# Value projection of two heads at once by halves, and the output's drain moved to ScalarE a turn later, in a two-layer transformer kernel

## The reference

```
q = x @ (wq_codes * scales) + bq;  k, v likewise          # 256 -> 16 x 128
scores = einsum("bqhd,bkhd->bhqk", q, k) / sqrt(128)
attn   = softmax(scores);  out = einsum("bhqk,bkhd->bqhd", attn, v)
return (out @ (wo_codes * wo_scales)) + bo
```

## Time and profile before

| | |
|---|---|
| time, median of 3 runs | 1179.99 us (1179.53 to 1180.14) |
| profiled execution, its own time | 1189.32 us |
| its span | 1187.5 us |
| PE, DVE, ACT, POOL busy | 88%, 63%, 47%, 24% of the span |
| chain that ended last, by engine | PE 65%, DVE 19%, issue 6%, ACT 5%, DMA 3% |
| second attention, first matmul to start of the output projection | 634.84 to 923.48 us |

### The profile page before, as it was taken

One profiled execution on the slowest core, in us unless ns is written; L12 is line 12 of the kernel. 1 busy time (PEld: TensorE's weight loads), 2 busy tenths in 40 slices (PEclk: granted clock), 3 DMA queues, 4 the chain that ended last, 5 costly groups with the idle time before them and its releaser, 6 DMA issues.

```text
span 1187.5 us, 16824 instructions
## 1 busy us (share of the span) xinstructions
PE 1043.6 (88%) x5771; PEld 819.4 (69%) x5771; DVE 750.1 (63%) x1275; ACT 552.7 (47%) x1081; POOL 285.7 (24%) x243
## 2 busy tenths in 40 slices
PE   6788999999999959847976999999997997669986
PEld 4567888888888844323434988998897454458775
DVE  1378998998989819953125787778776134523344
ACT  1056777777778648910113555555554021122220
POOL 0004234243243310022002112211210005336560
PEclk8589999999999969968997999999998998689997
DMA  7037778777677760060001111111100102168744
GB/s 259 1 86 155 165 157 167 156 158 173 153 152 168 186 139 10 1 186 9 0 0 46 36 54 53 45 34 53 53 0 0 67 1 75 52 204 257 248 154 183
DMA packets 77373, 121.59 MB, mean 102 GB/s; under 512 B 25027, under 2 KB 54414, under 8 KB 76560
## 3 DMA queue, kind: packets, MB, share of 16 engines
q1 hardware_dynamic: 65296, 86.91, 24.1%
q0 software_dynamic: 12032, 34.11, 15.0%
HBM read 70.31 MB, written 38.08 MB: 91 GB/s over the span
## 4 chain that ended last, share of the span: by engine, by line
PE 65%; DVE 19%; issue 6%; ACT 5%; DMA 3%; POOL 1%; DVEq 1%; another core or an unknown queue 0%; POOLq 0%; ACTq 0%; SPq 0%
PE psum L604 7%; PE psum L606 7%; PE psum L605 7%; PE psum L838 5%; PE psum L964 5%; DVE arena L1313 4%; PE psum L924 4%; PE psum L627 4%; PE psum L811 3%; PE psum L704 3%; PE psum L656 2%; DVE arena L1408 2%; PE psum L974 2%; PE psum L757 2%; PE psum L589 2%
## 5 line engine op out<-in xcount | busy, mean ns | idle before, releaser
L1313 DVE SCALAR_TENSOR_TENSOR arena<-arena,par_in 128x1024 f32<-128x1024 f32 x144 | 184.6, 1284 | 40.4 <-ACT arena L1041 28.2
L604 PE MATMUL psum<-lut_w_r,arena_r 128*128 128x512 f32 x320 | 132.0, 413 | 17.0 <-POOL arena_r L1739 10.1
L605 PE MATMUL psum<-lut_w_r,arena_r 128*128 128x512 f32 x320 | 127.7, 399 | 0.0
L606 PE MATMUL psum<-lut_w_r,arena_r 128*128 128x512 f32 x320 | 127.6, 399 | 0.0
L1723 POOL DMA_DIRECT2D arena<-arena x64 | 53.8, 983 | 216.5 <-DVE arena L1325 216.4
L1142 ACT ACTIVATE arena<-psum,small 128x256 f32<-128x256 f32 x128 | 59.4, 473 | 85.8 <-DVE small L1450 85.8
L1031 ACT ACTIVATE arena<-psum 128x1024 f32<-128x1024 f32 x48 | 49.3, 1027 | 73.9 <-PE psum L606 73.4
L604 PEld LDWEIGHTS psum<-lut_w_r,arena_r 128*128 128x128 f32 x320 | 61.3, 192 | 30.2 <-issue 10.1
L604 PE MATMUL psum<-arena_r 128*128 128x256 f32 x256 | 77.7, 304 | 1.5 <-DVE arena_r L1475 1.5
L1770 POOL DMA_INDIRECT out_rows<-arena x64 | 62.8, 981 | 51.6 <-issue 20.8
L1739 POOL TENSOR_TENSOR arena_r<-arena,arena_r 128x512 fp32r<-128x512 f32 x16 | 21.2, 1325 | 216.9 <-ACT arena_r L1153 216.9
(11 more groups left out here) (228 smaller groups left out, 2404.0 us busy)
## 6 DMA issues: line engine op xcount, KB each, us to landing
arena<-arena POOLq DMA_DIRECT2D x64, 256.0 KB, 5.6
arena<-in_w_moe SPq DMA_DIRECT2D x33, 384.0 KB, 7.2
slot_rows<-nowhere SPq DMA_DIRECT2D x16, 576.0 KB, 4.3
arena<-slot_rows SPq DMA_DIRECT2D x32, 288.0 KB
arena<-bands SPq DMA_DIRECT2D x16, 528.0 KB, 4.4
sq_rows<-arena POOLq DMA_DIRECT2D x16, 512.0 KB, 7.3
arena<-in_w_qkvz SPq DMA_DIRECT2D x16, 384.0 KB, 3.3
arena<-in_qkv_codes SPq DMA_DIRECT2D x16, 384.0 KB, 3.2
```

Of the source, the lines that this page charges most:

```text
L604: nc.tensor.matmul(dst, w_l, x_h, start=start, stop=False, skip_group_check=True)
L605: nc.tensor.matmul(dst, w_h, x_l, start=False, stop=False, skip_group_check=True)
L606: return nc.tensor.matmul(dst, w_h, x_h, start=False, stop=stop, skip_group_check=True)
L1313: nc.vector.scalar_tensor_tensor(by_batch(dst), by_batch(u[s])[:, :, j:j + S], par_in[:, bass.ds(M_CW + (w * H + h) * TAPS + j, 1)], by_ba ...
```

## The change

- v is projected by halves, for two heads (even and odd, side by side in 256 columns) at once, and for half of the tokens in each turn: 4 token tiles x 2 x 3 matmuls of 256 columns, the input as the stationary operand. The pair of heads 2i and 2i + 1 is made in turns 2i and 2i + 1; the output of head 2i, in turn 2i + 1, needs both halves. `z_half(par, zq)` says which half of the tokens and `zq` which set of buffers, as the first attention does for z.
- It comes first of the projections in a turn (behind scores 0 and 1); q then goes to `slot(1)`, k to `slot(0)`.
- v's weights have their own loads, product with the scales, and halves, once for two heads: `load_v` on SP (10 transfers), `weights_v` and `weights_v_lower` on POOL, `upper_v` on ACT. The halves lie in the space of `h_t`, which is no longer read.
- The output of head h-2 is taken out of `slot(1)` by ACT in turn h (stage 4), behind exponentials 0 and 1; DVE's drain is gone. There is one more turn, H + 1, for the last drain.
- ACT's copy of v is behind exponential 2, DVE's subtraction of v behind normalising 2.
- Scores 0 wait for all three lower halves of the head; the output waits for `pt_lower` batch by batch.

```diff
         def turns1(eng, turn):
-            turn(0, 0, 0, (1,))
-            turn(1, 0, 1, (1, 2))
-            with eng.Fori(1, H // 2) as i:
-                turn(2 * i, i, 0, (1, 2))
-                turn(2 * i + 1, i, 1, (1, 2))
-            turn(H, H // 2, 0, (2,))
+            turn(0, 0, 0, (1,), 0)
+            turn(1, 0, 1, (1, 2, 3), 0)
+            with eng.Fori(0, (H - 4) // 4) as i:
+                for j in range(2):
+                    turn(4 * i + 2 * j + 2, 2 * i + j + 1, 0, (1, 2, 4), 1 - j)
+                    turn(4 * i + 2 * j + 3, 2 * i + j + 1, 1, (1, 2, 3, 4), 1 - j)
+            turn(H - 2, H // 2 - 1, 0, (1, 2, 4), 1)
+            turn(H - 1, H // 2 - 1, 1, (1, 2, 4), 1)
+            turn(H, H // 2, 0, (2, 4), 0)
+            turn(H + 1, H // 2, 1, (4,), 0)
...
+            with sp.Fori(0, H // 2 - 1) as i:
+                sp.wait_ge(sg("a1_wmul"), 2 * i + 1)
+                load1(2 * i + 1)
+                sp.wait_ge(*at("a1_wv_lo", i + 1))
+                load_v(i + 1)
+                sp.wait_ge(sg("a1_wmul"), 2 * i + 2)
+                load1(2 * i + 2)
...
                 if 2 in st:
-                    pe.wait_ge(sg("a1_lo"), 3 * h - 1)
+                    pe.wait_ge(sg("a1_lo"), 3 * h)
                     scores(0)
                     scores(1)
                 if 1 in st:
-                    pe.wait_ge(sg("a1_w_lo"), h + 1)
-                    if since(h, 1):
-                        pe.wait_ge(sg("a1_lo"), 3 * h)
-                    project_by_halves(slot(0), par, 0).then_inc(sg("a1_q"), 1)
+                    pe.wait_ge(*at("a1_wv_lo", hh + 1))
+                    for t in range(HN):
+                        for k in range(KC):
+                            c, w = ...
+                            i = by_halves(slot(0)[:, t * 2 * P:(t + 1) * 2 * P], hh_h[:, c], hh_l[:, c], wv_h[:, w], wv_l[:, w],
+                                          k == 0, k == KC - 1)
+                    i.then_inc(sg("a1_v"), 1)
...
                 if 1 in st:
+                    pe.wait_ge(sg("a1_w_lo"), h + 1)
                     if since(h, 2):
                         pe.wait_ge(sg("a1_o_sb"), h - 1)
-                    project_by_halves(slot(1), par, 1).then_inc(sg("a1_k"), 1)
...
+                    project_by_halves(slot(1), par, 0).then_inc(sg("a1_q"), 1)
                     pe.wait_ge(sg("a1_lo"), 3 * h + 1)
-                    v_tiles(range(0, 3))
+                    project_by_halves(slot(0), par, 1).then_inc(sg("a1_k"), 1)
                 if 2 in st:
                     turned(2)
                     turned(3)
-                if 1 in st:
-                    v_tiles(range(3, NT)).then_inc(sg("a1_v"), 1)
-                if 2 in st:
-                    pe.wait_ge(sg("a1_lo"), 3 * h + 2 if 1 in st else 3 * h)
-                    pe.wait_ge(sg("a1_pt_lo"), 4 * h)
+                    if 1 in st:
+                        pe.wait_ge(sg("a1_lo"), 3 * h + 2)
                     for b in range(B):
+                        pe.wait_ge(sg("a1_pt_lo"), 4 * (h - 1) + b + 1)
...
# ACT
+                if 4 in st:
+                    act.wait_ge(sg("a1_o"), h - 1)
+                    nc.scalar.activation(G[:, bass.ds((h - 2) * T, T)], slot(1), ACT.Identity,
+                                         bias=...).then_inc(sg("a1_o_sb"), 1)
                 if 2 in st:
                     pt_upper(0)
                     expo(2)
+                if 1 in st:
+                    act.wait_ge(sg("a1_v"), h + 1)
+                    for e in range(2):
+                        i = nc.scalar.activation(by_tile(v_h[zq][e][...]),
+                                                 slot(0).rearrange("p (t e d) -> p e t d", e=2, d=P)[:, e], ACT.Copy)
+                    i.then_inc(sg("a1_hi"), 1)
+                if 2 in st:
                     pt_upper(1)
                     expo(3)
+                if 3 in st:
+                    upper_v(hh + 1)
...
+            def upper_v(i):
+                act.wait_ge(*at("a1_wv", i + 1))
+                nc.scalar.activation(wv_h, code_v, ACT.Copy).then_inc(sg("a1_wv_hi"), 1)
...
+            act.wait_ge(sg("in_lo"), 2 * KC)
+            upper_v(0)
...
# DVE: behind normed(2)
+                    dve.wait_ge(sg("a1_hi"), 3 * h + 1)
+                    for e in range(2):
+                        m = nc.vector.tensor_tensor(by_tile(v_l[zq][e][:, c]), slot(0).rearrange(...)[:, e],
+                                                    by_tile(v_h[zq][e][:, c].bitcast(F32)), ALU.subtract)
+                    m.then_inc(sg("a1_lo"), 1)
...
-                    dve.wait_ge(sg("a1_o"), h)
-                    nc.vector.tensor_scalar(G[:, bass.ds((h - 1) * T, T)], slot(1), ...).then_inc(sg("a1_o_sb"), 1)
...
# POOL
+            def weights_v(i):
+                pool.wait_ge(*at("a1_code_v", 160 * (i + 1)))
+                nc.gpsimd.tensor_tensor(code_v, code_v, scl_v, ALU.mult).then_inc(sg("a1_wv"), 1)
+
+            def weights_v_lower(i):
+                pool.wait_ge(*at("a1_wv_hi", i + 1))
+                nc.gpsimd.tensor_tensor(wv_l, code_v, wv_h.bitcast(F32), ALU.subtract).then_inc(sg("a1_wv_lo"), 1)
...
+                weights(2 * i + 1, 1)
+                weights_v(i + 1)
+                weights_lower(2 * i + 1, 1)
+                weights_v_lower(i + 1)
+                weights(2 * i + 2, 0)
+                weights_lower(2 * i + 2, 0)
```

More of the change, by code:

```diff
@@ L1156, in turn1 @@
                     expo(1)
[L1157 to L1160, removed]
+                if 4 in st:
+                    act.wait_ge(sg("a1_o"), h - 1)
+                    nc.scalar.activation(G[:, bass.ds((h - 2) * T, T)], slot(1), ACT.Identity,
+                                         bias=par_in[:, bass.ds(M_BQKV + 2 * H + h - 2, 1)]).then_inc(sg("a1_o_sb"), 1)
                 if 2 in st:
@@ L1173, in turn1 @@
                 if 1 in st:
-                    act.wait_ge(sg("a1_v"), h + 1)
-                    nc.scalar.activation(v_h[par], slot(0), ACT.Copy).then_inc(sg("a1_hi"), 1)
+                    act.wait_ge(sg("a1_k"), h + 1)
+                    nc.scalar.activation(k_h, slot(0), ACT.Identity, bias=par_in[:, bass.ds(M_BQKV + H + h, 1)])\
+                        .then_inc(sg("a1_hi"), 1)
+            def upper_v(i):
+                act.wait_ge(*at("a1_wv", i + 1))
+                nc.scalar.activation(wv_h, code_v, ACT.Copy).then_inc(sg("a1_wv_hi"), 1)
             for k in range(KC):
@@ L1460, in normed, with lower @@
                     m.then_inc(sg("a1_norm"), 1)
-                def lower(n, dst, src, upper, bias=None):
+                def lower(n, dst, src, upper, bias):
                     dve.wait_ge(sg("a1_hi"), 3 * h + n)
-                    if bias is None:
-                        m = nc.vector.tensor_tensor(dst, src, upper.bitcast(F32), ALU.subtract)
-                    else:
-                        m = nc.vector.scalar_tensor_tensor(dst, src, par_in[:, bass.ds(M_BQKV + bias, 1)], upper.bitcast(F32),
-                                                           ALU.add, ALU.subtract)
-                    m.then_inc(sg("a1_lo"), 1)
+                    nc.vector.scalar_tensor_tensor(dst, src, par_in[:, bass.ds(M_BQKV + bias, 1)], upper.bitcast(F32),
+                                                   ALU.add, ALU.subtract).then_inc(sg("a1_lo"), 1)
                 def pt_lower(b):
@@ L1482, in turn1 @@
                     normed(1)
-                if 1 in st:
-                    lower(1, q_l[par], slot(0), q_h[par], h)
                 if 2 in st:
@@ L1489, in turn1 @@
                     normed(2)
+                if 1 in st:
+                    dve.wait_ge(sg("a1_hi"), 3 * h + 1)
+                    for e in range(2):
+                        c = slice(z_half(par, zq) * 512, z_half(par, zq) * 512 + 512)
+                        m = nc.vector.tensor_tensor(by_tile(v_l[zq][e][:, c]), slot(0).rearrange("p (t e d) -> p e t d", e=2, d=P)[:, e],
+                                                    by_tile(v_h[zq][e][:, c].bitcast(F32)), ALU.subtract)
+                    m.then_inc(sg("a1_lo"), 1)
+                if 2 in st:
                     pt_lower(1)
@@ L1492, in turn1 @@
                 if 1 in st:
-                    lower(2, k_l, slot(1), k_h, H + h)
+                    lower(2, q_l[par], slot(1), q_h[par], h)
                 if 2 in st:
@@ L1497, in turn1 @@
                 if 1 in st:
-                    lower(3, v_l[par], slot(0), v_h[par])
-                if 2 in st:
-                    dve.wait_ge(sg("a1_o"), h)
-                    nc.vector.tensor_scalar(G[:, bass.ds((h - 1) * T, T)], slot(1), par_in[:, bass.ds(M_BQKV + 2 * H + h - 1, 1)],
-                                            None, ALU.add).then_inc(sg("a1_o_sb"), 1)
+                    lower(3, k_l, slot(0), k_h, H + h)
             turns1(dve, turn1)
+            dve.wait_ge(sg("a1_o"), H)
             for k in range(KC):
@@ L1745, in _ @@
             rstd_pool(pool, "n2")
```

(12 more changed lines are left out.)

66 lines of the change are left out of this document (35 added, 31 removed), and 2 rows, old and new, of the table REUSED.

## The result

The changed kernel is slower: 1.0054 of the kernel before, 95% interval 1.0034 to 1.0074 (medians 1188.78 and 1182.32 us of 20 runs each), so +6.4 us where +2.1 was forecast. A second comparison gave 1.0067 (1.0040 to 1.0094). Single executions of one kernel differ by some 12 us (before: 1174.4 to 1185.9). The two profiled executions show it the other way round, 1186.4 of span after and 1187.5 before, so their spans prove nothing.

A forecast was written before the change was run, and what follows sets the result against it. PE was taken to bound the stage; turns of 17.17 against 17.03 us gave +2.5, the opening +2.0 and the tail -2.4, so +2.1 on a median of 1179.99: 1182.1 us, range 1172 to 1188.

The forecast's parts named there:

- Costed at nothing: Stage and loads before it: POOL's products (at most 9.3 of 34 us), SP's transfers and first loads add no time.
- Opening: From the stage's start to turn 1's first transpose: +2.0 us, bounds +0.5 and +2.5.
- as POOL waits for the norm anyway: Ahead of the stage: first loads, first product of v's weights and their scales cost nothing.
- v's price: v in each turn: 24 half matmuls of 256 columns take 2.85 us for 3.49, 0.64 less PE work.
- The circle of waits: In each turn over PE, ACT and DVE: PE waits 0.56 us before k and 0.39 before the next scores.
- the whole gain of 0.97: PE work in a turn: 16.06 us without a wait, 0.97 less than now.
- the restarts: In each turn, where PE restarts after a wait: 0.08 us added each time, 0.16 in all.
- that clock term: Opening: slow matmuls (0.55 us the first) after 2.8 idle put turn 1's first transpose at 654.6, without them 653.0.
- Tail: Last turn's softmax and output: first transpose -0.6 us, output -1.65, ACT's drain -0.16; sum -2.4, bounds -1.2 and -3.5.
- 14 turns: Turn 1's first transpose to turn 15's: +2.0 us, with a turn of 17.17 against 17.03.
- stay the bound: Rival on the turns: ACT and DVE deliver v and k sooner, both waits gone, 1165.5 us (halved, 1175); chance 0.25.
- the clock's case: Rival on the stage: PE's idle of 0.95 a turn lowers the clock, 1192 us, or 1187 at half; chance 0.15.

The follow-up runs named there:

- the early transposes: Changed kernel with transposes of batch 2 put between q and k on PE; 1.0035 (1.0004 to 1.0066) to the kernel before.
- without the later products: Changed kernel making v's weights only for the first pair of heads and using them for all; 1.0021 (0.9990 to 1.0053) to the kernel before.

## Why the prediction was wrong

The step that failed is **Costed at nothing**: "POOL: ... at most 3 x 3.09 = 9.3 of 34". That POOL has time for its products is true (6.31 of 34.49 busy), and it doesn't matter. What counts is what DVE does while they run. Two kinds of DVE instruction stand still under a POOL product in these traces: a tensor_scalar out of SBUF into SBUF (normalising, h_t, a peak's scale) and a product of two SBUF tensors. Those that read PSUM don't, even where their second operand lies in SBUF (the subtraction of 1024 columns has 1.28 to 1.29 in 24 cases begun beside a product, 1.27 to 1.29 elsewhere), nor does the reciprocal. In a turn of the kernel before POOL's two products began at 748.8 and ended at 751.9, beside the output, the drain out of PSUM and the first peak, and met nothing that could be hurt. The change put new products into the queue ahead of old ones and so moved both into the normalising.

The trace that the prediction was made from had the collision in the stage's opening, between the last two of the earlier trace rows, and I had not read it:

```profile
648.46 1.84 POOL L1735 TENSOR_TENSOR arena<-arena 128x768 f32<-128x768 f32 x1
648.53 1.79 DVE L1450 TENSOR_SCALAR small<-small 128x2 f32<-128x2 f32 x1
```

In the turn of the earlier trace rows, at 752.14, behind POOL's product, the same scale takes 0.17.

**Opening, "as POOL waits for the norm anyway"**, the second half of the same step. That POOL stands idle before the norm is right, but behind it the wo product lies across DVE's writes of h_t. Its +3.3 us, and the 4.4 of collisions in the turns, are what was missed; terms below that came out smaller than forecast hid some 2 of it.

The terms that I did cost:
- v's price: 24 starts (650.50 to 653.20, 23 gaps) at 0.118 as in the first attention, 2.83 (taken 2.85). Right. The reason given, that 256 columns don't run at the pace of their columns alone, is not borne out: records of 512 columns step by 0.233, which is 0.117 for 256, so the short records lose next to nothing.
- *The circle of waits.* From start to start 0.55 before k for 0.56, and 0.35 (brackets 0.19) to 0.46 (0.30) before the scores for 0.39. A turn without a collision is 17.00 to 17.11 for 17.17; before it is 17.03. That the whole gain of 0.97 goes into these waits and the restarts was right, and the early transposes, 16.62, bear out the circle.
- *Opening* +0.9 + 0.7 = +1.6 for +2.0, in part by luck. PE started 0.9 later and not 1.3: POOL's lower half took 1.26, not the 1.78 of 632.92, where it had begun beside DVE's product of two SBUF tensors. Then v took 5.26 at a granted clock of 0.50 (635.19 to 640.45), 1.1 more than I had counted. And the idle of 2.52 before turn 1's scores was there, but no slow matmuls followed (0.38 for the first, where a first one in the last turn has 0.56; clock 1.00 from 649.0 to 653.3): that clock term did not come.
- *Tail* and last turn: 16.01 to 13.45 and 16.86 to 16.52, -2.9 for the -1.9 of the table. Right in kind, a third too small.
- *14 turns*: +5.6 for +2.0; without the later products +1.2. The missing 4.4 are the collisions: some 0.4 in each of seven odd turns, the rest in the two even ones of 18.02 and 17.90 and in one odd one of 17.62.

Sum by measured terms: 1.6 + 5.6 - 2.9 = +4.3 against the forecast +2.1, and +3.3 ahead of the feed-forward: 7.6.

The rivals: PE did not stay the bound (0.25), since both waits are there; the clock didn't fall (0.15), it is 1.00 from 652 to 900 us in both traces. That 1188.8 lies among the times of the clock's case is an accident; what made the time was not on the list. Of the distance to the forecast of 1182.1, 2.3 us are the kernel before itself, whose median is 1182.3 over 20 runs and was 1180.0 in the three shown. The page of the Trainium skill that bears on it ("SBUF — State Buffer", Who interferes with whom) says that POOL and DVE share a pair of ports, that a tensor_scalar on SBUF alone can take both ports, or an instruction with two SBUF inputs the second one, and that whichever of the two engines starts first keeps them for its whole instruction while the other stands still. The traces agree: 0.62 to 2.71 with POOL the first by 0.03 and 0.11, and the product of two SBUF tensors at the norm, `L302 TENSOR_TENSOR arena<-cst,small`, takes 2.27 beside POOL in the changed kernel and 2.81 in the one before (there L298), for 1.23 alone in the stage's own norm. I had left that rule out of the prediction and looked at POOL's busy share alone.

## What to carry to other kernels

Before moving or adding a POOL product, write down which DVE instructions run in its time. Here each tensor_scalar within SBUF and each product of two SBUF tensors waited for its end, those that read PSUM and the reciprocals didn't. An idle engine is not a free place; hold the product with a semaphore of the consumer stage until DVE is at PSUM work. And when work goes into a queue, follow what was behind it to the end of the kernel: here a load of the next stage moved a product across another stage's norm.

## What the runs showed of the hardware that I had not expected

A DVE instruction held up by POOL waits whole: two of 0.35 became 1.41 and 1.38 under two products of 1.3 that follow each other without a gap, each waiting out one of them, and a peak's scale of two elements took up to 1.23 for 0.17 in the changed kernels, and 1.79 once in the opening of the kernel before. POOL loses little by that: its products of 512 columns are 1.28 to 1.35 there and 1.25 to 1.30 elsewhere, and the wo product is 8.82 in the changed kernel, where DVE waits at it for six microseconds, and 8.81 where it was held until DVE had written h_t.

It works the other way round too, where DVE is the one that is already running. In the kernel before the wo product takes 9.79: it begins at 531.16, while DVE's product of two SBUF tensors (529.46, held until 531.19) runs until 532.27. In the changed kernel that DVE product runs until 527.88, v's product begins beside it at 526.76, and it is now v's that takes 2.23 for 1.31 alone, and wo 8.82. Each loses the same 0.9 to 1.0. Where the wo product begins behind that instruction's end, at 527.85 with only the drain moved, it is 8.83.
